# Score products on 64 rows, issued in pairs into two banks, in a decoder block on one core

## What is computed

```python
def step(S, qkv):
    qi, ki, vi = qkv
    scores = jnp.einsum('bthd,bshd->bhts', qi, ki) * D[None]
    o_intra = jnp.einsum('bhts,bshd->bthd', scores, vi)
    o_inter = jnp.einsum('bthd,bhde->bthe', qi * decay_q[None, :, :, None], S)
    S_new = lam_C[None, :, None, None] * S + jnp.einsum('bshd,bshe->bhde', ki * decay_k[None, :, :, None], vi)
    return (S_new, o_intra + o_inter)
```

## Time and profile before

| | us |
|---|---|
| median of 3 runs | 222.52 |
| lowest and highest of these | 221.6, 222.95 |
| the profiled execution | 220.85 |
| its span, first to last instruction | 219.0 |

### The profile page before, as it was taken

How to read it: one execution, slowest core, us unless ns; L and a number is a source line. 1 busy time by engine, 2 the same in 40 slices (tenths; PEclk the granted TensorE clock), 3 DMA queues, 4 the chain that set the end, 5 groups by cost and what they waited for, 6 DMA issues and landing times.

```text
span 219.0 us, 3542 instructions
## 1 busy us (share of the span) xinstructions
PE 176.8 (81%) x1066; PEld 116.9 (53%) x1066; DVE 152.9 (70%) x437; ACT 91.4 (42%) x229; POOL 107.0 (49%) x190
## 2 busy tenths in 40 slices
PE   1999999999999999999999228999963199950670
PEld 1678565565545565666987118679632045530440
DVE  0246999898798988889764007428629996999961
ACT  0365477185372736612342113454640146620233
POOL 9957389132334613220553156112268757584663
PEclk9999999999999999999999857999999569997587
DMA  6999015200000000023027582010211001000012
GB/s 199 305 321 372 35 49 199 92 4 0 19 7 3 24 4 24 0 67 131 5 98 259 192 249 65 0 49 3 96 48 48 24 1 48 1 3 0 0 48 96
DMA packets 16370, 17.46 MB, mean 80 GB/s; under 512 B 3024, under 2 KB 13792, under 8 KB 16352
## 3 DMA queue, kind: packets, MB, share of 16 engines
q1 hardware_dynamic: 13424, 14.57, 20.2%
q0 software_dynamic: 768, 2.10, 3.0%
q10 hardware_dynamic: 2160, 0.56, 1.3%
HBM read 7.79 MB, written 5.77 MB: 62 GB/s over the span
## 4 chain that ended last, share of the span: by engine, by line
PE 66%; DVE 12%; POOL 7%; issue 6%; DMA 3%; ACT 3%; SPq 1%; POOLq 0%; DVEq 0%
PE bank L1398 26%; PE bank L1476 13%; PE bank L1632 5%; PE bank L1393 5%; PE bank L1617 5%; PE bank L1499 4%; POOL yg L412 3%; PE bank L1494 2%; PE bank L1519 2%; DMA x_sb<-in_x 2%; DMA ys_d<-qkr 2%; PE bank L1507 2%; DVE w_qk L1165 1%; POOL rstd L365 1%; DVE newton L914 1%
## 5 line engine op out<-in xcount | busy, mean ns | idle before, releaser
L1476 PE MATMUL bank<-qx,kT 128*128 128x512 f32 x64 | 32.7, 608 | 0.0
L1398 PE MATMUL bank<-f_w,oT 128*128 128x512 f32 (+4 forms) x80 | 29.1, 515 | 2.3 <-ACT oT L688 2.2
L619 ACT ACTIVATE qx<-bank,con 32x256 f32<-32x256 f32 x64 | 26.4, 460 | 7.6 <-PE bank L1393 5.1
L947 DVE TENSOR_TENSOR probs<-bank,con 128x512 f32<-128x512 f32 x32 | 21.8, 686 | 3.4 <-PE bank L1476 3.2
L1398 PEld LDWEIGHTS bank<-f_w,oT 128*128 128x128 f32 x80 | 15.2, 200 | 13.5 <-issue 7.1
L348 POOL TENSOR_TENSOR rsin<-qk,rope_tab 128x256 f32<-128x256 f32 x16 | 13.2, 846 | 13.4 <-ACT qk L598 13.4
L356 POOL TENSOR_TENSOR on<-ogs,ors 128x256 f32<-128x256 f32 x8 | 5.4, 679 | 24.9 <-DVE ors L916 24.9
L362 POOL TENSOR_SCALAR rstd<-agg 128x1 f32<-128x1 f32 x24 | 6.1, 254 | 21.5 <-DVE agg L983 20.2
L1398 PE MATMUL bank<-w_qk,xT 128*128 128x512 f32 x32 | 15.2, 596 | 0.0
L1617 PE MATMUL bank<-xsT,slot_w 128*128 128x128 f32 x112 | 15.1, 291 | 0.0
L1632 PE MATMUL bank<-slot_w,rsin 128*128 128x256 f32 x56 | 13.6, 383 | 1.5 <-DVE rsin L1064 1.5
(11 more groups left out here) (151 smaller groups left out, 396.9 us busy)
## 6 DMA issues: line engine op xcount, KB each, us to landing
slot_w<-ctxT SPq DMA_DIRECT2D x14, 256.0 KB, 2.5
xs_d<-xs SPq DMA_DIRECT2D x2, 896.0 KB, 8.3
xs<-xs_d SPq DMA_DIRECT2D x6, 256.0 KB, 3.1
ys_d<-qkr SPq DMA_DIRECT2D x6, 256.0 KB, 2.3
x_sb<-in_x SPq DMA_DIRECT2D x4, 256.0 KB, 6.9
ctx_sb<-in_ctx SPq DMA_DIRECT2D x1, 1024.0 KB, 10.9
out<-x_sb SPq DMA_DIRECT2D x8, 128.0 KB, 1.7
con<-shape_constants SPq DMA_DIRECT2D x1, 402.5 KB, 3.2
```

The lines of the kernel that those rows point to most:

```text
L619: eng.activation(qx[rr, i % 2, :, 2 * r + par, :], two(bank[2][rr, 0:2 * P]), ACT.Copy, scale=con[rr, C_PARITY + par:C_PARITY + par + 1]). ...
L947: eng.tensor_tensor(probs[:, i % 2, 4 * g:4 * g + 4, :], bank[3 + g % 2][:, :].rearrange("p (h n) -> p h n", h=4), causal.unsqueeze(1).to_ ...
L1398: last = eng.matmul(dst, lhsT[:, k, :], w[:, k, :], start=(k == 0), stop=(k == KT - 1))
L1476: eng.matmul(bank[3 + g % 2][:, :], kT[:, i % 2, g // 2, :], qx[:, i % 2, g // 2, 4 * (g % 2):4 * (g % 2) + 4, :].rearrange("p h n -> p (h ...
```

## The change

Two products on 64 rows take the place of two on 128. Rows 0 to 63 of half f hold the heads 8f to 8f+3, rows 64 to 127 the heads 8f+4 to 8f+7. scores(i, f) now issues two products, one on each 64 rows, into banks 3 and 4. The first waits for the mask two before it, the second for the mask just before it. qx has four copies on all 128 rows; in copy n the rows of the heads with h % 4 = n are not zero, by a column of the constants (C_HEAD), so it takes no memset, and expand_q has 4 instructions on 128 rows. As a copy now carries two heads of a half, the state must be zero on the rows of the other four heads: decay_state writes 4 blocks of 128 columns with a factor that is zero on the other 64 rows (C_CHUNK has 4 columns). fq, which lay in qx, gets a tile of its own. The lists of all engines but SP's are in another order; no call is added or dropped but the scores calls, 16 in place of 32.

```diff
-        qx = sb("qx", [P, 2, KT, 8, P])
+        qx = sb("qx", [P, 2, KT, 4, P])
...
-        fq = after[:, 0:1024].rearrange("p (c l n) -> p c l n", c=2, l=L)
-        fv = after[:, 2048:4096].rearrange("p (c l n) -> p c l n", c=2, l=L)
+        fq = sb("fq", [P, 2, L, P])
+        fv = after.rearrange("p (c l n) -> p c l n", c=2, l=L)
...
-                eng.memset(qx[:, :, :, :, :], 0.0).then_inc(S_("zeros"), 1)
...
-                for r in range(4):
-                    rr = slice(32 * r, 32 * r + 32)
-                    for par in range(2):
-                        eng.activation(qx[rr, i % 2, :, 2 * r + par, :], two(bank[2][rr, 0:2 * P]), ACT.Copy,
-                                       scale=con[rr, C_PARITY + par:C_PARITY + par + 1]).then_inc(S_("q_expanded"), 1)
+                for n in range(4):
+                    eng.activation(qx[:, i % 2, :, n, :], two(bank[2][:, 0:2 * P]), ACT.Copy,
+                                   scale=con[:, C_HEAD + n:C_HEAD + n + 1]).then_inc(S_("q_expanded"), 1)
...
-                    eng.tensor_scalar(state[:, b, f, :], bank[7][:, f * D:(f + 1) * D], con[:, C_CHUNK + f:C_CHUNK + f + 1],
-                                      None, ALU.mult).then_inc(S_("state"), 1)
+                    for half in range(2):
+                        n, a = 2 * f + half, half * P
+                        eng.tensor_scalar(state[:, b, f, a:a + P], bank[7][:, n * P:(n + 1) * P],
+                                          con[:, C_CHUNK + n:C_CHUNK + n + 1], None, ALU.mult).then_inc(S_("state"), 1)
...
-            def scores(i, g):
-                eng.wait_ge(S_("q_expanded"), 8 * i + 8)
+            def scores(i, f):
+                eng.wait_ge(S_("q_expanded"), 4 * i + 4)
                 eng.wait_ge(S_("kT_copied"), i + 1)
-                done = 4 * i + g
-                if done >= 2:
-                    eng.wait_ge(S_("probs"), done - 1)
-                else:
-                    eng.wait_ge(S_("ctxT_copied"), 4)
-                eng.matmul(bank[3 + g % 2][:, :], kT[:, i % 2, g // 2, :],
-                           qx[:, i % 2, g // 2, 4 * (g % 2):4 * (g % 2) + 4, :].rearrange("p h n -> p (h n)"),
-                           start=True, stop=True).then_inc(S_("scores_made"), 1)
+                for half in range(2):
+                    done = 4 * i + 2 * f + half
+                    if done >= 2:
+                        eng.wait_ge(S_("probs"), done - 1)
+                    else:
+                        eng.wait_ge(S_("ctxT_copied"), 4)
+                    rows_ = slice(64 * half, 64 * half + 64)
+                    eng.matmul(bank[3 + half][:, :], kT[rows_, i % 2, f, :],
+                               qx[rows_, i % 2, f, :, :].rearrange("p h n -> p (h n)"),
+                               start=True, stop=True).then_inc(S_("scores_made"), 1)
...
-                                   qx[:, i % 2, h // 8, h % 8, :], start=True, stop=False)
+                                   qx[:, i % 2, h // 8, n, :], start=True, stop=False)
```

More of the change, by code:

```diff
@@ L76, in shape_constants @@
     c[:, C_DECAY + H:C_DECAY + 2 * H] = np.exp(-slope[None, :] * (64.0 - p[:, None]))
[L77 to L78 removed]
+    for n in range(4):
+        c[:, C_HEAD + n] = p // HD % 4 == n
     c[:, C_ROPE2:C_ROPE2 + L * 2 * HK] = rope(-np.arange(L), HK).reshape(1, -1)
@@ L1564, in attention_round @@
                     proj_v(i + 1)
-                for g in range(4):
-                    scores(i, g)
+                for f in range(KT):
+                    scores(i, f)
                 if 0 <= i - 2:
@@ L1715, in _ @@
-            transpose_x(7)
             proj_gate(4)
-            rank_tokens()
             proj_gate(5)
+            proj_v(1)
+            turn_k(0)
+            turn_q(0)
+            proj_qk(2)
             proj_gate(6)
             proj_gate(7)
-            proj_qk(1)
-            turn_k(0)
+            make_state(0)
             turn_expert(0)
             turn_expert(1)
-            proj_qk(2)
+            proj_qk(3)
+            turn_k(1)
             turn_expert(2)
-            turn_q(0)
@@ L1743, in _ @@
+            turn_k(2)
             attend(0, 3)
-            scores(1, 0)
+            turn_q(2)
+            proj_qk(5)
+            scores(1, 1)
             turn_back(0)
-            scores(1, 1)
-            scores(1, 2)
-            turn_k(2)
-            scores(1, 3)
-            turn_q(2)
-            proj_qk(4)
-            make_state(2)
             attend(1, 0)
             attend(1, 1)
+            scores(2, 0)
+            make_state(2)
+            scores(2, 1)
             attend(1, 2)
+            attend(1, 3)
@@ L1756, in _ @@
+            turn_k(3)
+            turn_q(3)
             proj_v(3)
-            transpose_on(0)
-            turn_q(3)
-            scores(2, 0)
-            project_o(0)
-            scores(2, 1)
-            attend(1, 3)
-            scores(2, 2)
-            turn_back(1)
             attend(2, 0)
             attend(2, 1)
-            scores(2, 3)
-            proj_v(4)
-            attend(2, 2)
-            turn_k(3)
-            proj_qk(5)
-            make_state(3)
-            turn_q(4)
@@ L1774, in _ @@
-            scores(3, 0)
-            scores(3, 1)
-            attend(2, 3)
-            proj_qk(6)
-            transpose_on(1)
-            scores(3, 2)
-            attend(3, 0)
-            turn_k(4)
-            turn_back(2)
-            scores(3, 3)
-            turn_k(5)
+            proj_qk(6)
+            turn_q(4)
+            attend(2, 2)
+            make_state(3)
+            proj_qk(7)
+            turn_back(1)
+            transpose_on(0)
+            turn_k(4)
+            project_o(0)
@@ L1785, in _ @@
+            turn_k(5)
+            proj_v(4)
+            scores(3, 0)
+            attend(2, 3)
+            turn_back(2)
+            attend(3, 0)
+            turn_q(5)
+            proj_v(5)
+            transpose_on(1)
+            scores(3, 1)
+            project_o(1)
             scores(4, 0)
-            project_o(1)
-            proj_qk(7)
-            scores(4, 1)
-            proj_v(5)
             attend(3, 1)
@@ L1792, in _ @@
             attend(3, 3)
-            turn_q(5)
-            scores(4, 2)
+            scores(4, 1)
+            turn_back(3)
             attend(4, 0)
-            turn_back(3)
-            scores(4, 3)
-            turn_k(6)
             attend(4, 1)
-            turn_k(7)
             turn_q(6)
-            transpose_on(2)
-            scores(5, 0)
-            project_o(2)
-            proj_v(6)
             attend(4, 2)
             attend(4, 3)
-            scores(5, 1)
-            attend(5, 0)
-            scores(5, 2)
-            turn_back(4)
-            transpose_on(3)
-            scores(5, 3)
+            proj_v(6)
+            turn_k(6)
+            scores(5, 0)
+            transpose_on(2)
+            turn_q(7)
+            turn_k(7)
+            project_o(2)
+            turn_back(4)
+            attend(5, 0)
+            transpose_on(3)
+            scores(5, 1)
+            proj_v(7)
+            project_o(3)
+            scores(6, 0)
             attend(5, 1)
-            proj_v(7)
-            scores(6, 0)
-            turn_q(7)
             attend(5, 2)
```

344 lines of the change are left out of this document (169 added, 175 removed).

## The result

The kernel after takes 225.39 us in the median (224.71 to 226.89, 4 runs), the kernel before beside it 222.29. The ratio is 1.0149, 95% interval 1.0087 to 1.0212: 3.1 us slower, where 216.0 was forecast and 212.0 to 223.5 was the range.

A forecast was written before the change was run, and what follows sets the result against it. TensorE's full list to 122.6 us was taken as the bound: 13.7 us saved by overlap, less 3.7 for shape changes and 2 of waits, allows 8; 6.5 was taken off 222.52, giving 216.0 us, range 212 to 223.5.

The forecast's parts named there:

- The bound: First half, to 122.6 us: ends when TensorE is through its list; the relay of slot products behind it brings the second half forward.
- signs of being right: Trace after: score products in couples, two records per 0.43 us; VectorE over 88% from 33 us; relay's last store near 117.
- The overlap: Score products on TensorE: the two of a pair run fully beside each other, 0.86 us a pair, saving 13.7 us.
- C: Rival, score pairs: half an overlap, three slots of 0.43 us per pair instead of two; 220.5 us, chance 0.17.
- D: Rival, score pairs: no overlap, 1.72 us streamed as before plus 3.7 for entries and exits; 225.5 us, chance 0.18.
- 0.17 per switch: TensorE changing array shape around tiled blocks: 13 more switches cost 2.2 us, 3.7 together with 1.5 for weight loads.
- The second product's wait: TensorE, score pairs: the second product waits for the mask just before it; some 2 us in all, bounds 0 and 8.
- The lists: Reordered queues of all engines: every instruction still there, so on a full TensorE the order moves nothing; 0 us.
- TensorE's saving as time: First half: TensorE's side allows 8 us, VectorE's 8.0; both can't be full with in-order lists, so 6.5 taken.
- Rival B: VectorE takes over: masks in bursts of two, TensorE stalls half a microsecond at each pair; 219.5 us, chance 0.13.
- The second half: Behind the relay, some ten places of the lists reordered: 0 us, bounds -1.5 and +1.5.
- Zeros, state, ScalarE: Dropped qx memset worth 0 to 0.5 us, state blocks 1.4 us more VectorE work, ScalarE 13 us less, worth nothing itself.

The follow-up runs named there:

- experiment 3: The kernel after with the second half of its lists, from slots_down(3), activate(3), copy_ys(3) and gather(3) on, as in the kernel before: 224.26 us.
- experiment 7: Eight calls moved in pairs' old lists, 218.94 us; eight in new lists, 219.52; rearranged pairs with pair_weights(4) moved, 214.16; their first half with old second half, 212.52.
- experiment 5: The kernel after with both score products of a pair on rows 0 to 63, so they can't overlap (values wrong): 238.17 us, ratio 1.0479.
- experiment 6: Lists rearranged by single calls with a queue model: pairs of the kernel after 214.32 us; as control, products of the kernel before 223.49 us.
- experiment 4: The kernel after with one VectorE call moved, mark_experts() behind copy_xT(5): 224.8 us, ratio 1.0147.

## Why the prediction was wrong

**The bound.** Right: TensorE's list and the relay at its end set the first half. Over all the runs the relay ends between 113.9 and 146.5 us, and the rest behind it is 94.9 to 99.5. Of the signs of being right the pair's own came, while VectorE was busy 77% from 33.5 us to the relay where over 88% was forecast, and the last store came at 126.04, not near 117.

**The overlap.** Right, and C and D are out: a whole pair takes 1.06 us. The terms were 0.86 and 0.1 for the entry, with 0.17 per switch; 0.20 in the pair and 0.19 around it were measured, 0.39 for a pair and its two switches where 0.44 was reckoned. The Trainium skill ("TensorE: Matmul & The Clock Gate", Part 3: Packing small matmuls) has products start and end in program order. As whole products the two of a pair agree with that, 7 ns apart; taken of their passes too, it would make a pair 1.29 us, and the measurement decides for 1.06.

**The second product's wait.** Forecast some 2 us. The pairs take 20.9 us, 3.9 over sixteen whole ones; 0.7 of it is one pair in a stretch of the low clock (71.52 us, 1.78). Between scores(6, 1) and (7, 0), priced at 1.3 us, 1.4 went (0.9 idle, and a second pair of 1.56 instead of 1.06). In the new lists the term was 1 us short. What it missed is that it isn't a property of the pair: in the old lists it is 7 us (24.2 against 17), with eight calls moved 3, with fitted lists 0.4.

**The lists: the step that failed.** "Every instruction is still there, so on a full TensorE the order moves nothing." TensorE was full because its order left it full; with another order it isn't. TensorE did get less to do: up to the start of slots_down(3) it was busy 109.5 us where it had been 115.0, and 107.8 in experiment 3, where the clock didn't drop. But over the same calls it was idle 9.8 us where it had been 1.6, and these 8.2 us are more than it had gained. Priced by runs, the new lists cost 3.4 us with pairs and 15 with single products. A rearranged list is a change with a price of its own and no row of the trace of before can show it; it had to be followed call by call, at least where TensorE's next work hangs on VectorE: mark_experts ahead of the copies of x, residual1(0) ahead of the copy that turn_k(5) waits for. I had all of it: the lists, the rows and the durations.

**TensorE's saving as time.** "Two engines can't both be full with in-order lists" was said and priced at 1.5 us. In the old lists this is the whole of it, without any cost of new lists: with 5.2 us less of product time (24.2 for 29.3) and 13 us less on ScalarE, 0.0 us was gained, as the masks, and maybe other calls, stood where single products wanted them. With fitted lists 8 to 10 us came out, more than the 6.5 I took, with VectorE at 87% up to the relay.

**Rival B.** Its place was right, its form not. Time went into waits around masks and two banks, but not half a microsecond at each pair: a few places, each the work of the list. That moves of single calls gave 3.1 and 5.9 us, and fitted lists 11, shows that VectorE was not the bound.

**The second half.** Forecast 0, bounds -1.5 and 1.5. Measured 2.3 us more from the last store on in the two profiled executions; two pairs of runs (experiments 3 and 7) give 1.1 and 1.6 us for the order, each time with intervals that overlap. The last four slices of the page have TensorE at 1.2 GHz in the kernel after and at both levels in turn with the old order. The order doesn't fix the clock, though: with the same new second half, experiment 5 had a mean clock of 0.86 behind the relay and the shortest rest of all, 94.9, the kernel after 0.80 and 97.9; the kernel before had 0.83 and 95.7. Nor does the clock account for everything, since the rearranged pairs had 97.5 at 0.80 in experiment 6 and 99.5 at 0.81 in experiment 7. What the new order of the second half costs, and by which calls, stays open.

**Zeros, state, ScalarE.** The four copies of a query took 1.57 us where 1.7 was reckoned, the state's four blocks 1.11 where 1.2 was. Nothing showed of either, as forecast. That no engine but TensorE and VectorE mattered agrees with it, but wasn't shown alone.

## What to carry to other kernels

Where engines work through lists in a fixed order, the lists belong to the durations that they were made for: a cheaper instruction in an old list may give nothing, and a new list may cost more than the instruction saves. Price the two apart, old work in new lists and new work in old lists, and before calling a saving void, look for the few calls on which the idle places of the critical engine hang; here eight moves were worth as much as a third of the whole gain. An instruction that takes two buffers at once wants its consumers one step sooner than two that take one each.

## What the runs showed of the hardware

Two f32 products on disjoint 64 rows started 7 ns apart, and both first passes ran before both second passes: 36.38 and 36.91 above. A late second product cost just its lateness: when it started 0.24 us after the first, the pair took 1.29 (1.06 + 0.24), at 0.82 us 1.88. In the pair of 1.29 the second passes, too, started 0.24 us apart.

TensorE's clock did not fall in the same way in every execution of the same calls. After six microseconds of the first half in which TensorE was busy 3.8 to 4.1, it fell to 1.2 GHz in the kernel after, for 3.4 of the next 30 us (mean 0.94), and with products on one half of the rows for all of them (0.50), busy 29.28 of 30 us. In experiment 3, with the same first half as the kernel after, it didn't fall:

```profile
62.00:68.00 6.00, 3.72 (x31) 1.92 (x30) 4.80 (x16) 1.80 (x5) 1.51 (x3) 1.00 0.00 0
68.00:98.00 30.00, 27.26 (x308) 16.37 (x300) 25.33 (x80) 8.89 (x23) 8.77 (x13) 1.00 0.11 35
```

Nor did it in experiment 4 (3.86 of 6.00 us busy, then 1.00). Idle places can cost twice, in themselves and in the clock behind them, but the same idle places cost the clock in one execution and not in another; what decides it no run here shows. Before, the first 122.6 us ran at 1.00 throughout.
